# Maxima of the next head beside the scores of the running head: by key tiles in place of an even spread

## The chip, the cores and the metric

The kernel runs on one core of one Trainium2 chip. The metric is the device time of one execution in microseconds (us). The engines are TensorE (PE in the profile; PEld is its weight load), VectorE (DVE), ScalarE (ACT), GpSimd (POOL) and SyncE (SP), which issues DMAs.

## The reference, cut to what matters

The reference is one transformer block: a modulated layer norm, causal attention with 16 heads of 32 channels, a residual, and a mixture of experts. The part in question is the attention:

```python
B, T, C, H = (4, 2048, 512, 16)
qkv = x @ Wqkv.T + bqkv
q, k, v = (to_heads(z) for z in split(qkv, 3))
q, k = _rope(q), _rope(k)
att = jnp.einsum('bhqd,bhkd->bhqk', q, k) * scale
att = jnp.where(causal, att, -jnp.inf)
att = jax.nn.softmax(att, axis=-1)
y = jnp.einsum('bhqk,bhkd->bhqd', att, v)
```

The softmax needs the maximum of each query's row of scores before it can take exponentials.

## The kernel before, in words

**Batches and phases.** A loop runs over the 4 batches. In each, `front()` sets the order of the projections and `stream()` that of the attention; then comes the routing of tokens. The experts follow after all batches. `STEPS = front() + stream()` is one list of steps, and every engine walks the same list and does its own part of each step. So the list sets the order on each engine's in-order queue, and semaphores set the rest.

**Two passes over the scores of a head.** Scores are computed twice. In the first pass (`max` steps) the queries lie on the partitions: TensorE multiplies 128 queries by up to 512 keys into one of three PSUM banks `S1` (L1307), and VectorE reduces the bank to one maximum per query, with `reduce_max` (L1648) for whole tiles and with a masking operation (L1644) for the tiles on the diagonal, 128 to 512 wide. A head has 40 such tiles (`TILES`, `NTILE`), numbered by query block and then by chunk of 512 keys. After the 12th (`FIRST_HALF`) and the 40th, VectorE takes the maximum over chunks (`most`, L1654, it writes `mx`), TensorE transposes it (`row`, L1312, also into an `S1` bank), VectorE writes it negated to `mT` (`negated`, L1663), and SyncE copies it by a DMA (`max_row`, L736) into a row of `QK`. So the maximum is subtracted inside the second pass's matmul.

In the second pass (`score` steps) the keys lie on the partitions: TensorE multiplies 128 keys by 512 queries into one of three banks `S2` (L1330, with a masking matmul L1333 on the diagonal), and ScalarE takes the exponential into `Pt` (L1137). These 40 key tiles are taken in 15 rounds of two or three (`ROUNDS`, `NR`): rounds 0 and 1 (2 tiles each) belong to query chunk 0, rounds 2 to 4 (3, 2, 3) to chunk 1, rounds 5 to 8 (3 each) to chunk 2, rounds 9 to 14 (3, 3, 3, 3, 2, 2) to chunk 3. `ROUND_OF` gives the round of a tile. GpSimd adds the exponentials of a round (`plus`, L1002, into `Sm`), and TensorE multiplies them by the values (`value`, L1354, L1357, L1358), which also sums the denominators.

**The order.** `stream()` fills `beside`, a list of steps for each round of each head. Rounds are taken two at a time: one tile's score, then one step of `beside` of these two rounds, and so on until both are used up; then the two `plus`, then the two `value` steps of the two rounds before, then `closing` (copies of a finished chunk, and for every fourth head the joining of parts on GpSimd and the reciprocals of the denominators on VectorE, L1596). As 15 is odd, an even head's stretches begin at rounds 0, 2, 4 and so on, an odd head's at rounds 1, 3, 5, and the stretch "14, 0" holds the last round of an even head and the first of the odd one.

**Waits.** A `max` or `row` step on TensorE waits until the step three before it on the same bank has been read (L1261, L1263). A `row` waits for `most` (L1311). The scores of rounds 0 and 5 wait for the DMA of the row of their half (L1318). Q and K of head h+1 are brought by twelve DMAs (`stack`) that are issued once the scores of head h-1 are done, and the first `max` tiles of a chunk wait for theirs (L1306).

**Where the maxima stand before.** The maxima of head h are spread evenly over rounds of head h-1: for h = 1 over 12 steps from round 4, for later heads over 14 steps from round 2, three in most rounds and two in some. `most` comes one round after the last maximum of its half, `row` and `negated` two rounds after.

Of the kernel before, what the change touches and what calls it, by code (L numbers as in the profile page):

```python
# [89 lines left out]
NTILE = len(TILES)  # L90
SHAPES = ((2, 2), (3, 2, 3), (3, 3, 3, 3), (3, 3, 3, 3, 2, 2))
ROUNDS = [(j, tuple(range(sum(shape[:r]), sum(shape[:r + 1])))) for j, shape in enumerate(SHAPES) for r in range(len(shape))]
NR = len(ROUNDS)
# [13 lines left out]
def tile_at(j, k):  # L107

    return 2 * j * (j + 1) + k
# [7 lines left out]
ROUND_OF = {tile_at(j, k): r for r, (j, ks) in enumerate(ROUNDS) for k in ks}  # L117
# [34 lines left out]

FIRST_HALF = sum(qb < NT // 2 for qb, _, _ in TILES)
LAST_CHUNK = sum(qb < NT - TPC for qb, _, _ in TILES) + 8
TILES_FROM = 2
FIRST_TILES_FROM = 4
OUT_AT = (10, 10, 11, 12, 13, 14, 15, 16)


def stream():  # L160

    closing = [[] for _ in range(NR * H + 12)]
    beside = [[] for _ in range(NR * H)]
    negated = {}
    for i in range(LAST_CHUNK, NTILE):
        beside[(i - LAST_CHUNK) // 4].append(("max", 0, i))
    beside[2].append(("most", 0, 1))
    beside[3] += [("row", 0, 1), ("negated", 0, 1)]
    for hh in range(1, H):
        late = TILES_FROM if hh > 1 else FIRST_TILES_FROM  # L170
        at, span = NR * (hh - 1) + late, NR + 1 - late
        for i in range(NTILE):
            beside[at + i * span // NTILE].append(("max", hh, i))
            if i in (FIRST_HALF - 1, NTILE - 1):
                half, n = int(i >= FIRST_HALF), at + i * span // NTILE
                beside[n + 1].append(("most", hh, half))
                beside[n + 2].insert(0, ("row", hh, half))
                negated[n + 2] = ("negated", hh, half)
    for n, step in negated.items():
        beside[n].insert(2, step)  # L180
    for hh in range(H):
        for j in range(NCH):
            n = NR * hh + LAST_ROUND[j] + LAG
            closing[n].append(("copy", hh, j))
            if hh == H - 1 and j < NCH - 1:
                closing[n + 2] += [("join", NG - 1, j), *(("inverse", NG - 1, j, i) for i in range(TPC))]
                closing[n + 3].append(("scale", NG - 1, j))
            elif hh % GH == GH - 1 and hh < H - 1:
                closing[n + 3].append(("join", hh // GH, j))
                for i in range(TPC):  # L190
                    closing[n + 3 + i // 2].append(("inverse", hh // GH, j, i))
                closing[n + 5].append(("scale", hh // GH, j))
    last = NR * (H - 1)
    for i, t in enumerate(OUT_AT):
        closing[last + t].append(("out", *divmod(i, TPC)))
        if i == TPC - 1:
            closing[last + t].append(("moments",))
    closing[last + NR].append(("normed",))
    closing[NR * (H - 3)].append(("fold",))
    closing[last - 1].append(("widen", 0))  # L200
    closing[last + 5].append(("widen", 1))
    out = []
    for n in range(0, NR * H + 12, 2):
        if n < NR * H:
            here = [divmod(n, NR), divmod(n + 1, NR)]
            tiles = [("score", hh, r, k) for hh, r in here for k in ROUNDS[r][1]]
            aside = beside[n] + beside[n + 1]
            for i in range(max(len(tiles), len(aside))):
                out += tiles[i:i + 1] + aside[i:i + 1]
            out += [("plus", *of) for of in here]  # L210
        if 2 <= n < NR * H + 2:
            out += [("value", *divmod(n - 2, NR)), ("value", *divmod(n - 1, NR))]
        out += closing[n] + closing[n + 1]
    return out
# [8 lines left out]


STEPS = front() + stream()
USES = [step for step in STEPS if step[0] in ("max", "row")]
EMPTIED = {step: n + 1 for n, step in enumerate(step for step in STEPS if step[0] in ("max", "vproj"))}
# [1652 lines left out]
```

## Time and profile before

| | us |
|---|---|
| median of 3 runs | 4263.35 |
| lowest, highest | 4261.73, 4266.28 |
| the profiled execution | 4274.07 |
| its span, from first to last instruction | 4272.3 |

| engine | busy us | share of the span |
|---|---|---|
| TensorE matmuls | 3856.6 | 90% |
| VectorE | 2747.9 | 64% |
| ScalarE | 1806.0 | 42% |
| GpSimd | 2783.0 | 65% |

The mean granted clock of TensorE is 0.946 of 2.4 GHz. The profile is one execution. Matmuls are pipelined and their ends are modelled, so the start-to-start distance of two matmuls says more than their length: a matmul of 512 columns is 0.40 us long in the rows while the next starts 0.23 us later. A wait in a row stands in brackets with what ended it; on TensorE it is shorter than the distance between the two starts.

### The profile page before, as it was taken

The page shows a single profiled execution, that of the slowest core. Times are in us where ns is not written, and L with a number is a line of the kernel's source. Part 1 is how long each engine was busy: PE and PEld are TensorE (multiplying, and loading weights), DVE is VectorE, ACT ScalarE, POOL GpSimd, SP SyncE. Part 2 cuts the span into 40 slices and gives each one's busy share as a digit, 9 for nine tenths or more (in the row PEclk, how much of TensorE's full clock was granted, in tenths as well). Part 3 has the DMA queues.
Part 4 walks back from the last instruction along what each step waited for, and adds up shares of the span by engine and source line. Part 5 has one row for each costly group of instructions (what it writes and reads, how often), then busy time and mean ns, then how long its engine had stood idle before and what let it go on. Part 6 is the DMA issues. An engine that isn't in the chain of part 4 may idle for free. (4 is left out here: it accounts for less than half of the span.)

```text
span 4272.3 us, 80797 instructions
## 1 busy us (share of the span) xinstructions
PE 3856.6 (90%) x21344; PEld 2337.9 (55%) x21344; DVE 2747.9 (64%) x5841; ACT 1806.0 (42%) x3526; POOL 2783.0 (65%) x2251
## 2 busy tenths in 40 slices
PE   5989999987999999878899999879899999859998
PEld 2754544456744454457554454457545544547776
DVE  3767677466757767476667776467676774645655
ACT  1345555523355555332355555233455554311111
POOL 3768788824668879716678888427687888115554
PEclk8989999998999999989899999889999999979999
DMA  6533333243533333334433333425433332349997
GB/s 211 178 120 90 92 98 106 81 174 105 175 97 100 83 102 99 120 135 147 140 91 98 101 96 108 156 72 180 123 91 91 100 106 85 103 126 258 257 258 190
DMA packets 305439, 549.11 MB, mean 129 GB/s; under 512 B 59877, under 2 KB 99941, under 8 KB 301797
## 3 DMA queue, kind: packets, MB, share of 16 engines
q1 hardware_dynamic: 283496, 485.62, 37.8%
q0 software_dynamic: 21504, 58.40, 5.9%
q8 instruction: 183, 3.00, 0.3%
q14 instruction: 256, 2.09, 0.2%
HBM read 311.86 MB, written 174.85 MB: 114 GB/s over the span
## 5 line engine op out<-in xcount | busy, mean ns | idle before, releaser
L1137 ACT ACTIVATE Pt<-PS 128x512 f32<-128x512 f32 (+3 forms) x2560 | 1205.2, 542 | 1003.0 <-PE PS L1330 557.5
L1002 POOL TENSOR_TENSOR Sm<-Pt 128x512 f32<-128x512 f32 (+3 forms) x960 | 1028.4, 1077 | 389.2 <-ACT Pt L1137 383.2
L1648 DVE TENSOR_REDUCE part<-PS 128x1 f32<-128x512 f32 x1536 | 1004.2, 685 | 335.6 <-PE PS L1307 330.5
L1307 PE MATMUL PS<-QK 96*128 96x512 f32 (+3 forms) x2560 | 1026.6, 419 | 84.1 <-DVE mT L1663 24.8
L1330 PE MATMUL PS<-QK 97*128 97x512 f32 (+3 forms) x2560 | 994.2, 410 | 40.8 <-DMA QK<-mT 20.9
L1354 PE MATMUL PS<-Pt,V 128*32 128x512 f32 (+3 forms) x5120 | 874.4, 556 | 37.1 <-POOL Sm L1002 36.9
L1358 PE MATMUL PS<-Sm,onesv 128*32 128x512 f32 (+3 forms) x1920 | 823.2, 537 | 0.0
L1644 DVE CUSTOM_DVE_ANT_0 PS<-PS,consts 128x128 f32<-128x128 f32 (+3 forms) x1024 | 504.0, 495 | 411.1 <-PE PS L1307 403.8
L1330 PEld LDWEIGHTS PS<-QK 97*128 97x128 f32 x2560 | 489.6, 194 | 478.3 <-issue 349.6
L1002 POOL TENSOR_TENSOR Sm<-Sm,Pt 128x512 f32<-128x512 f32 (+1 forms) x640 | 712.4, 1113 | 50.2
L1307 PEld LDWEIGHTS PS<-QK 96*128 96x128 f32 x2560 | 496.0, 195 | 292.3 <-DVE part L1648 107.6
L1354 PEld LDWEIGHTS PS<-Pt,V 128*32 128x32 f32 x5120 | 218.5, 111 | 364.5 <-issue 243.3
L1291 PE MATMUL PS<-hTu,W 128*128 128x512 f32 x1024 | 327.9, 402 | 25.2 <-DVEq L644 13.4
L976 POOL TENSOR_TENSOR t<-qraw,cs 128x1024 f32<-128x1024 f32 x64 | 183.7, 2870 | 171.3 <-ACT qraw L1102 162.1
L1038 POOL DMA_INDIRECT out<-z,it x96 | 138.9, 1447 | 214.9 <-issue 111.8
L1596 DVE RECIPROCAL den<-den 128x128 f32<-128x128 f32 x256 | 221.2, 914 | 73.6 <-DMA den<-od 72.1
L1456 PEld LDWEIGHTS PS<-XT,Wg 128*96 128x96 f32 x1536 | 251.6, 164 | 27.0 <-issue 25.4
L1456 PE MATMUL PS<-XT,Wg 128*96 128x192 f32 x1536 | 260.5, 328 | 1.3 <-ACT XT L1188 1.3
L1333 PE MATMUL PS<-mtbf,idbf 128*128 128x128 bf16 (+1 forms) x1024 | 238.7, 236 | 0.0
L1291 PEld LDWEIGHTS PS<-hTu,W 128*128 128x128 f32 x1024 | 194.4, 193 | 72.4 <-issue 17.1
L1124 ACT ACTIVATE od<-PS 128x512 f32<-128x512 f32 x256 | 155.8, 609 | 138.5 <-PE PS L1358 138.5
L1102 ACT ACTIVATE qraw<-PS,bqg 128x512 f32<-128x512 f32 x128 | 87.0, 680 | 284.3 <-PE PS L1291 248.5
(169 smaller groups left out, 4945.7 us busy)
## 6 DMA issues: line engine op xcount, KB each, us to landing
QK<-qkd SPq DMA_DIRECT2D x720, 128.0 KB, 3.1
qkd<-st SPq DMA_DIRECT2D x64, 1024.0 KB, 4.5
Wg<-wgu SPq DMA_DIRECT2D x48, 768.0 KB, 5.0
o<-od SPq DMA_DIRECT2D x448, 64.0 KB, 2.0
W<-wd SPq DMA_DIRECT2D x3, 6144.0 KB, 21.5
Wd<-wdn SPq DMA_DIRECT2D x48, 384.0 KB, 6.0
xin<-x SPq DMA_DIRECT2D x16, 1024.0 KB, 7.8
vd<-vst SPq DMA_DIRECT2D x16, 1024.0 KB, 6.2
```

Source lines behind the costliest of these rows:

```text
L1002: nc.gpsimd.tensor_tensor(total, of[0][:, first:CH] if i == 1 else total, of[i][:, first:CH], ALU.add).then_inc(sum_done, 1)
L1137: nc.scalar.activation(Pt[:, t % NPT, first:CH], S2[t % NS2][:, first:CH], ACT.Exp, scale=SCALE).then_inc(exp_done, 1)
L1291: last = mm(bank, W[:, w, k, i, g * P:(g + 1) * P], (hTu, hTl)[h][:, j % 2, k], start=(k, w, h) == (0, *TERMS[0]), stop=(k, w, h) == (KT - ...
L1307: mm(s1[:, 0:w], QK[0:3 * HD, hh % 2, 0, qb * P:(qb + 1) * P], QK[0:3 * HD, hh % 2, 1, c * CH:c * CH + w], start=True, stop=True).then_inc ...
L1330: last = mm(S2[t % NS2][:, first:CH], QK[0:3 * HD + 1, hh % 2, 1, k * P:(k + 1) * P], QK[0:3 * HD + 1, hh % 2, 0, j * CH + first:(j + 1) * ...
L1333: last = mm(S2[t % NS2][:, first:first + masked], idbf[:, :], mtbf[:, 2 * P - masked:2 * P], start=False, stop=True)
L1354: mm(O[j % 2][i * HD:(i + 1) * HD, firsts[i]:CH], V[:, g % 2, k, h * HD:(h + 1) * HD], of[i][:, firsts[i]:CH], start=begins, stop=r == LAS ...
L1358: mm(O[j % 2][3 * HD:P, firsts[1]:CH], onesv[:, :], Sm[:, at % NSM, firsts[1]:CH], start=begins, stop=r == LAST_ROUND[j]).then_inc(pv_done, 1)
L1456: last = mm(banks[i][:, q, :], Wg[:, u % HELD, k, o:o + HALF], XT[:, u % 2, k // 2, k % 2, :], start=k == 0, stop=k == KT - 1)
L1596: v.reciprocal(den[:, cols], den[:, cols]).then_inc(den_inv, 1)
L1644: v.tensor_tensor_reduce(out=s1[:, 0:w], in0=s1[:, 0:w], in1=K[:, K_NEG + CH - w:K_NEG + CH], scale=1.0, scalar=-3e38, op0=ALU.add, op1=AL ...
L1648: v.reduce_max(part[:, qb, cc:cc + 1], s1[:, 0:w], AX.X).then_inc(s1_dve, 1)
```

## The change

For heads from 2 on, maximum i of head h goes to the round that holds tile i + 4 of head h-1 (`AHEAD`), so that there is one maximum for each score; the last four fall into rounds 0 and 1 of head h itself. For head 1 the maxima keep their even spread. For all heads from 1 on `most` stands in the round of the last maximum of its half and no longer in the next, and `row` and `negated` one round after it and no longer two. The rows are put in after all maxima are placed, at the head of their round. For heads from 2 on this gives, for the first half, the last maximum in round 6 in place of 5, for the second half in round 1 of the next head in place of round 0; the rows stay in the rounds 7 and 2. For head 1 `most` and the rows stand a round earlier.

```diff
-TILES_FROM = 2
-FIRST_TILES_FROM = 4
+AHEAD, FIRST_TILES_FROM = 4, 4
...
-    negated = {}
+    negated, rows_at = {}, []
...
     for hh in range(1, H):
-        late = TILES_FROM if hh > 1 else FIRST_TILES_FROM
-        at, span = NR * (hh - 1) + late, NR + 1 - late
         for i in range(NTILE):
-            beside[at + i * span // NTILE].append(("max", hh, i))
+            if hh == 1:
+                n = FIRST_TILES_FROM + i * (NR + 1 - FIRST_TILES_FROM) // NTILE
+            else:
+                past, tile = divmod(i + AHEAD, NTILE)
+                n = NR * (hh - 1 + past) + ROUND_OF[tile]
+            beside[n].append(("max", hh, i))
             if i in (FIRST_HALF - 1, NTILE - 1):
-                half, n = int(i >= FIRST_HALF), at + i * span // NTILE
-                beside[n + 1].append(("most", hh, half))
-                beside[n + 2].insert(0, ("row", hh, half))
-                negated[n + 2] = ("negated", hh, half)
+                half = int(i >= FIRST_HALF)
+                beside[n].append(("most", hh, half))
+                rows_at.append((n + 1, hh, half))
+    for n, hh, half in rows_at:
+        beside[n].insert(0, ("row", hh, half))
+        negated[n] = ("negated", hh, half)
     for n, step in negated.items():
         beside[n].insert(2, step)
```

As the code then emits them, the stretch of rounds 1, 2 of an odd head reads before and after (S score, M maximum of the head running ahead, tile numbers behind):

```
before  S.2 most S.3 row  S.0 M0  S.1 negated S.2 M1 M2
after   S.2 M38 S.3 M39  S.0 most  S.1 row  S.2 M0 negated M1 M2
```

## Rows read from the trace of the kernel before

**Rows 1.** The page, part 1: busy us (share) of each engine, xinstructions

```profile
PE 3856.6 (90%) x21344; PEld 2337.9 (55%) x21344; DVE 2747.9 (64%) x5841; ACT 1806.0 (42%) x3526; POOL 2783.0 (65%) x2251
```

**Rows 2.** TensorE's waits: who <- for whom: us in total, times, longest

```profile
PE PS L1354 <- POOL Sm L1002: 36.9, 25, 4.5
...
PE PS L1307 <- DVE mT L1663: 24.8, 33, 0.9
PE PS L1307 <- DVE part L1644: 24.4, 45, 1.3
PE PS L1330 <- DMA QK<-mT: 20.9, 4, 5.5
```

**Rows 3.** Windows: us, busy by engine, PEclk, DMA, GB/s; three of heads 4, 5

```profile
1329.95:1333.15 3.20, 3.20 (x30) 2.23 (x26) 2.16 (x5) 1.66 (x4) 3.12 (x5) 1.00 0.80 203
...
1368.35:1373.53 5.18, 3.76 (x28) 2.02 (x26) 1.60 (x7) 2.73 (x6) 1.35 (x2) 1.00 0.67 189
...
1397.26:1402.50 5.24, 5.03 (x34) 2.14 (x30) 3.56 (x7) 1.60 (x4) 4.58 (x5) 1.00 0.43 102
```

**Rows 4.** Groups by line, weight loads: xcount, busy us, mean ns, idle before

```profile
L1307 PEld LDWEIGHTS PS<-QK 96*128 96x128 f32 x2560 | 496.0, 195 | 292.3 <-DVE part L1648 107.6 <-DVE part L1644 66.8 <-DVE mT L1663 46.7
```

**Rows 5.** Timeline, TensorE, rounds 12, 13: start, us, operation, xcount [wait]

```profile
1359.39 0.40 PE L1307 MATMUL PS<-QK 96*128 96x512 f32 x1
1359.62 0.40 PE L1330 MATMUL PS<-QK 97*128 97x512 f32 x1
```

**Rows 6.** Timeline, VectorE, to the end of rounds 14, 0 (head 6)

```profile
511.52 1.88 DVE L1648 TENSOR_REDUCE part<-PS 128x1 f32<-128x512 f32 x3
513.32 0.69 DVE L1644 CUSTOM_DVE_ANT_0 PS<-PS,consts 128x512 f32<-128x512 f32 x1
...
514.11 0.19 DVE L1654 TENSOR_REDUCE mx<-part 128x8 f32<-128x32 f32 x1
```

**Rows 7.** Timeline, TensorE, rounds 13, 14 (head 5), the last maxima

```profile
1399.08 1.63 PE L1307 MATMUL PS<-QK 96*128 96x384 f32 x3
1400.65 0.63 PE L1354 MATMUL PS<-Pt,V 128*32 128x512 f32 x3
```

**Rows 8.** Timeline, TensorE, rounds 2, 3 (head 4), the last maxima

```profile
1335.22 0.98 PE L1307 MATMUL PS<-QK 96*128 96x384 f32 x3
1336.51 0.33 PE L1307 MATMUL PS<-QK 96*128 96x128 f32 x1 [0.30 <-DVE part L1644]
1336.87 0.62 PE L1354 MATMUL PS<-Pt,V 128*32 128x512 f32 x2
```

**Rows 9.** Timeline, TensorE, rounds 6, 7 (head 4), the last maximum

```profile
1347.32 0.39 PE L1307 MATMUL PS<-QK 96*128 96x256 f32 x1 [0.85 <-DVE mT L1663]
```

**Rows 10.** Timeline, TensorE, rounds 13, 14 (head 3), a value

```profile
1328.96 0.63 PE L1354 MATMUL PS<-Pt,V 128*32 128x512 f32 x3 [1.25 <-POOL Sm L1002]
```

**Rows 11.** Windows, rounds 1, 2, heads 3 to 13: one, the 24's sum

```profile
514.55:518.18 3.63, 3.63 (x27) 2.13 (x25) 1.61 (x7) 2.73 (x6) 1.22 (x2) 1.00 0.76 216
...
sum 102.54, PE 91.97 PEld 48.74 DVE 38.46 ACT 65.72 POOL 46.81; mean PE 3.83 PEld 2.03 DVE 1.60 ACT 2.74 POOL 1.95
```

**Rows 12.** Timeline, all engines, the first head's rounds 2, 3

```profile
1175.31 0.19 DVE L1654 TENSOR_REDUCE mx<-part 128x8 f32<-128x32 f32 x1
...
1175.55 0.38 PE L1312 MATMUL PS<-consts,mx 128*8 128x128 f32 x1 [0.43 <-DVE mx L1654]
```

**Rows 13.** Timeline, TensorE, rounds 1, 2 (head 5), the third maximum

```profile
1371.73 0.44 PE L1307 MATMUL PS<-QK 96*128 96x384 f32 x1
```

**Rows 14.** Timeline, TensorE, rounds 3, 4 (head 13), a value

```profile
746.32 0.63 PE L1354 MATMUL PS<-Pt,V 128*32 128x512 f32 x3 [1.37 <-POOL Sm L1002]
```

**Rows 15.** Windows, rounds 3, 4 of head 5, first batch

```profile
446.39:451.70 5.31, 5.31 (x33) 3.10 (x31) 3.28 (x9) 2.83 (x6) 3.55 (x4) 0.80 0.31 82
```

**Rows 16.** Windows, rounds 9, 10 of head 3 in two batches

```profile
383.66:391.33 7.67, 6.42 (x34) 3.15 (x30) 7.57 (x14) 3.26 (x6) 7.11 (x8) 0.78 0.12 27
...
1311.90:1318.21 6.31, 5.07 (x34) 2.66 (x31) 6.31 (x13) 3.20 (x6) 6.15 (x7) 1.00 0.16 36
```

## The prediction

> **What bounds the kernel now.** I began with the page. TensorE is busy 90% of the span, the next engines 65% and 64% [rows 1], and most of its work is the stream of attention. So the place to look is what TensorE waits for there. The list of waits gives little: 24.8 us for `negated` (L1663), 24.4 us for the diagonal maxima (L1644), 36.9 us for GpSimd's sums, and 20.9 us for a row's DMA, in four waits [rows 2]. Better placed maxima can't take away much more than the first two.
>
> Next I cut the stream into stretches of two rounds, as the code emits them (scores and maxima mixed, then two values): fifteen for two heads. In heads 4 and 5 of the second batch all run at full clock, and the reader is to see that lengths follow counts: 4 scores with 2 maxima take 3.20 us, 4 with 6 take 5.24 [rows 3]. So I price each stretch by itself. One maximum more or less on an unstalled TensorE I take as 0.235 us: its weight load is 0.195 us whatever the width [rows 4], the bound from below, and the wait-free steps from maximum to score in a run of full ones are 0.23 (1359.39 to 1359.62 [rows 5]). On VectorE a full maximum costs 0.60 us, for three follow each other in 1.88 and a fourth begins 1.80 behind the first, though one is 0.69 long [rows 6]. So on a run of maxima VectorE is the slower, with three PSUM banks between the two.
>
> The Trainium skill, "TensorE: Matmul & The Clock Gate", section "Wait — 56ns, not 53.3ns?", gives a matmul's spacing as columns over 2.4 GHz plus 2.5 ns, 56 ns for a 128-wide one. By it, dropping a 128-wide maximum would return 0.06 us and not 0.235; the trace has no such spacing between two maxima of the stream. No other sentence uses it.
>
> **The change part by part.** The maxima of a pair of heads' stretches become 4 5 6 6 6 6 5 4 (first, even head) and 5 5 6 6 6 6 4, in place of 2 6 6 6 5 6 6 5 and 3 6 6 5 6 6 6. From head 2 on the last maximum of a half falls one round later, its row in the round it had. No operation is added or removed. Per batch seven even heads (2 to 14) and seven odd ones (1 to 13) change, and head 15 at its start.
>
> *Stretches that shorten.* (a) Rounds 13, 14: the last three maxima take 1.57 us up to the value, because two wait for banks; without two of them the value stands some 0.6 behind: 0.97 less [rows 7]. (b) Rounds 2, 3: the sixth maximum waits until 1336.51 and the value begins at 1336.87; the fifth is the last of three that begin at 1335.22 and take 0.98, so it starts at about 1335.7, and without the sixth the value stands 0.43 behind it: 0.7 less [rows 8]. (c) Rounds 6, 7: `negated` lies behind a full maximum and holds a bank, 0.85 us of idle time [rows 9]; a 128-wide one takes that place, but a full one more stands ahead of `most`: 0.34 less. (d) One maximum less in rounds 12, 13, in 14, 0 and in 3, 4: 0.25 each. *That lengthen.* (e) Rounds 0, 1: two more, 0.46. (f) Rounds 8, 9: one more, 0.28. (g) Rounds 7, 8: one more, and the last now waits for the bank of a full one: 0.55. Rounds 4, 5, 5, 6, 9 to 12 keep their count: nothing.
>
> *Where the cover is gone.* In heads 3, 7, 11 GpSimd also joins the group's parts, and a value in rounds 13, 14 waits 1.25 us for its sum [rows 10]: there (a) and (g) come to nothing, the wait for GpSimd takes their place. In heads 4, 8, 12 reciprocals stand ahead of `negated`: (b) is half.
>
> Per batch: even heads -7 x 0.34 (c) - 7 x 0.5 (d) + 7 x 0.46 (e) + 7 x 0.28 (f) - 4 x 0.7 - 3 x 0.35 (b) = -4.6; odd heads -7 x 0.25 (d) - 4 x (0.97 - 0.55) = -3.4. Together -8.0 us.
>
> *The added wait.* Rounds 1, 2 of odd heads. Before, `most` begins at 514.11 [rows 6], ahead of the stretch (514.55 to 518.18, 3.63 us [rows 11]), and the row goes out at 515.04 unhindered. After, both last maxima lie in this stretch. The first is made 0.27 in, VectorE takes it at 0.89 (0.6 behind, as ever), the second at 1.49; `most` begins 0.79 later (514.11 against 513.32 [rows 6]) and ends at 2.47; the row, behind three scores in TensorE's queue, goes at 2.52, though TensorE is free at 1.45. That a row starts 0.05 behind the end of `most` is seen in the first head [rows 12]. Behind it wait a score and three maxima; `negated` comes behind the first of these and frees the third's bank at 3.87. From that third maximum to the end it is 1.80 us, as in head 5 (1371.73 to 1373.53 [rows 13]): 5.67. Before, these 24 stretches (heads 3 to 13) took 102.54 us, 4.27 each [rows 11]: in some the next head's first maximum waits for its DMA, and that wait is now hidden. So +1.40 x 6, and +1.2 in head 15: +9.6 per batch. Bounds for one: 5.3 (if VectorE is quicker to the last maxima) and 6.0.
>
> *What takes it up.* In head 13 a value of rounds 3, 4 waits 1.37 us for GpSimd, which folds the output weights [rows 14]; in head 15 it waits likewise. A later TensorE finds these done: -1.3 and -1.2. Head 5's falls of the clock behind its DMA wait go too: two of four stretches of rounds 3, 4 took 5.3 us at a lower clock [rows 15] and not 4.4, so -0.5. Sum per batch: -8.0 + 9.6 - 3.0 = -1.4, in four -6 us.
>
> *The clock.* In rounds 9, 10 of heads 3, 7, 11 TensorE idles for a maximum, 1.3 us at the longest [rows 2]. Nine of these twelve stretches show a lower granted clock (0.78: part of the stretch at 1.2 GHz) and take some 7.67 us, three stay at 2.4 GHz and take 6.31: 1.37 dearer [rows 16]. The new idle time is 1.07 us at the row and 0.5 at the bank, among narrow matmuls. I take a fall in two of three: 16 x 1.37 = 22, less 2 for falls that go. Bounds: 0 and 24 x 1.37 = 33.
>
> *Queues.* SyncE issues a row's DMA behind twelve for Q and K, and behind it the copies of the head before; it waited for `negated` before and still does. TensorE waits for a row's DMA four times, once in each batch, in the first head [rows 2], whose rows don't move. In even heads the way from the last score of the head before to the score that needs the row shrinks by 1.2 us (the terms a, b, e), in odd heads it grows. I put nothing; if the even ones had no slack it would be 7 x 4 x 1.2 = 34 us, but then some of today's heads would wait too.
>
> Total: -6 + 20 = +14 us. The profiled execution took 4274.07 us (span 4272.3), 10.7 above the median of the runs; the sum is a difference, and on the median it gives 4263 + 14, some 4276.
>
> **Rivals.** (1) *The clock holds.* If the idle time in rounds 1, 2 doesn't lower it, -6 us stays: 4257. For it: rounds 1, 2 of head 5 took 5.18 us with a long DMA wait, at full clock [rows 3]. Against it: [rows 16]. The Trainium skill, same page, "HAM oscillation — how this bites in real kernels", asks for longer idle gaps than these before the clock falls; by it this rival would be the forecast. (2) *The row hardly waits.* If rounds 1, 2 take 5.3 and (b) and (c) return the whole of their waits (0.5 more in 28 stretches), 24 x 0.37 + 28 x 0.5 = 23 us go: 4253 from the forecast, 4234 from rival 1. It decides where VectorE reaches a maximum clearly less than 0.6 us behind TensorE; no row shows that. (3) *GpSimd takes the gain in all heads.* In rounds 13, 14 it is busy 4.58 of 5.24 us without holding TensorE [rows 3]; at 4.27 it would, and 0.31 of 0.97 is lost, 16 x 0.31 = 5 us; with a fall of the clock in all 24 (11 more) this gives 4292, and if the whole 0.97 is lost 4302. (4) *Nothing to be told*: a maximum moved is one placed elsewhere, and the waits only change place: 4263.
>
> **How the numbers follow.** Forecast 0.5, rival 1 0.2, rival 2 0.1, rival 3 0.15, rival 4 0.05. The range, 4252 to 4294, leaves out the far parts of 2 and 3. Less than 0.2% (8.5 us) can't be told from no change. Faster (under 4254.8): rival 2 and part of 1, 0.18. Within: the rest of 1, rival 4 and the low side of the forecast, 0.27. Slower (over 4271.9): 0.55.
>
> **What would show it.** Right: a wait of the row's transpose for `mx`, about 1.0 us, in odd heads 3 to 15 and hardly elsewhere in the stream; rounds 1, 2 at 5.4 to 6.0 us at full clock; a lower granted clock behind about two thirds of them; rounds 13, 14 at 4.3 in heads 1, 5, 9, 13; rounds 0, 1 at 3.65; the wait for `negated` in rounds 6, 7 under 0.6; the DMA wait for Q and K gone. Wrong: if the clock stays up the sum is 20 us too high, and if rounds 1, 2 stay near 4 us another 35.

## The result, and the profile after

The changed kernel takes 4313 us in the median (4296 to 4317 in four runs, 4314 in four further ones), the kernel before 4264 to 4268: slower by a ratio of 1.0095 (95% interval 1.008 to 1.011), in the later comparison 1.0112 (1.0086 to 1.0139). The direction was forecast, the size was not: +47 to +49 us where I had +14, and outside the range, whose end was 4294.

The first profiled run of the changed kernel, 4295.94 us (span 4294.1), is the quickest of the eight, with a mean granted clock of 0.945. Most of its runs have 0.940 to 0.942. So I took a second trace, of a run of 4315.98 us at 0.940 (E5), and one of the kernel before at 4270.86 us and 0.948 (E6, its first had 0.946 and 4274.07). "First" and "second trace" below mean these. A "fall" is a stretch of two rounds whose granted clock (the PEclk column) is below 1.00; a "place" is one such stretch in one head and batch.

TensorE's waits after the change, first trace, columns as in [rows 2]; lines from L1307 on stand four further down than before:

```profile
PE PS L1358 <- POOL Sm L1006: 55.4, 47, 4.5
...
PE PS L1316 <- DVE mx L1658: 27.6, 32, 1.2
...
PE PS L1311 <- DVE part L1648: 15.3, 17, 1.2
...
PE PS L1311 <- DVE mT L1667: 13.5, 24, 0.9
...
PE PS L1311 <- DVE part L1652: 11.8, 39, 0.8
...
PE PS L1311 <- DMA QK<-qkd: 2.8, 5, 0.8
```

The reader is to see two things. The waits that the change aimed at shrank ([rows 2]: `negated` 24.8 to 13.5, the diagonal maxima 24.4 to 15.3), though the wait for whole tiles grew from 4.4 to 11.8, and a new one stands there, the row's transpose for `mx`, 27.6 us. The wait for a head's DMA went from 10.5 us to 2.8. And GpSimd's sums went from 36.9 us in 25 waits to 55.4 in 47.

The stretches of two rounds in heads 4 and 5 of the second batch, to be laid beside [rows 3]; in order rounds 0, 1, then 8, 9 of head 4, and 1, 2, then 3, 4, then 7, 8, then 13, 14 of head 5:

```profile
1336.10:1339.82 3.72, 3.72 (x33) 2.47 (x29) 2.69 (x7) 1.73 (x4) 3.64 (x5) 1.00 0.79 212
...
1354.87:1359.82 4.95, 4.95 (x34) 2.42 (x32) 4.28 (x10) 2.62 (x6) 4.87 (x5) 1.00 0.24 57
...
1373.98:1379.68 5.70, 4.25 (x29) 2.37 (x27) 3.09 (x11) 2.90 (x6) 2.25 (x4) 1.00 0.69 182
1379.68:1383.71 4.03, 4.03 (x33) 2.33 (x31) 2.55 (x8) 2.72 (x6) 2.86 (x4) 1.00 0.46 120
...
1388.49:1394.26 5.77, 5.56 (x35) 2.78 (x34) 3.43 (x10) 2.90 (x7) 5.61 (x6) 1.00 0.13 33
...
1403.77:1408.11 4.34, 4.24 (x33) 1.67 (x29) 2.42 (x5) 1.60 (x4) 4.26 (x5) 1.00 0.39 88
```

Rounds 1, 2 take 5.70 us (5.67 forecast) and rounds 13, 14 take 4.34 (4.27). TensorE's timeline in rounds 1, 2 of head 5 has both new waits in it, at the row and at a bank:

```profile
1374.99 0.63 PE L1334 MATMUL PS<-QK 97*128 97x512 f32 x2
1376.51 0.27 PE L1316 MATMUL PS<-consts,mx 128*8 128x128 f32 x1 [0.89 <-DVE mx L1658]
...
1377.88 0.44 PE L1311 MATMUL PS<-QK 96*128 96x384 f32 x1 [0.57 <-DVE mT L1667]
```

and VectorE's has the chain that makes the row late, two maxima of 0.6 us and then `most`:

```profile
1374.87 0.69 DVE L1652 TENSOR_REDUCE part<-PS 128x1 f32<-128x512 f32 x1 [1.72 <-PE PS L1311]
1375.48 0.69 DVE L1648 CUSTOM_DVE_ANT_0 PS<-PS,consts 128x512 f32<-128x512 f32 x1
...
1376.27 0.19 DVE L1658 TENSOR_REDUCE mx<-part 128x8 f32<-128x32 f32 x1
```

Two of the 24 stretches of rounds 1, 2, heads 3 to 13, first trace, and their sum:

```profile
1521.36:1528.13 6.77, 5.31 (x30) 2.57 (x28) 3.09 (x11) 2.90 (x6) 3.06 (x4) 0.84 0.77 206
...
3300.79:3308.42 7.63, 5.71 (x30) 2.77 (x28) 3.05 (x11) 2.94 (x6) 2.99 (x3) 0.73 0.63 171
...
sum 152.08, PE 116.42 PEld 59.69 DVE 74.02 ACT 69.83 POOL 78.97; mean PE 4.85 PEld 2.49 DVE 3.08 ACT 2.91 POOL 3.29
```

[rows 11] had 102.54 for these. With the wait, 11 stay at 1.00 and near 5.7 us, and 13 show a lower granted clock.

### The profile page after: what moved, and what is told of

Read it like the earlier page. It is cut to its first block and busy times, and to the rows that moved or that the text cites. A ratio compares the mean times of both kernels' runs of the same rounds, so it can differ in the third digit from the quotient of the medians.

```text
span 4294.1 us, 80797 instructions
## 1 busy us (share of the span) xinstructions
PE 3856.5 (90%) x21344; PEld 2340.2 (54%) x21344; DVE 2755.2 (64%) x5841; ACT 1807.1 (42%) x3526; POOL 2784.6 (65%) x2251
## 5 line engine op out<-in xcount | busy, mean ns | idle before, releaser
L1311 PE MATMUL PS<-QK 96*128 96x512 f32 (+3 forms) x2560 | 1036.8, 419 | 62.0 <-DVE part L1648 15.3
L1358 PE MATMUL PS<-Pt,V 128*32 128x512 f32 (+3 forms) x5120 | 879.8, 556 | 56.4 <-POOL Sm L1006 55.4
L1600 DVE RECIPROCAL den<-den 128x128 f32<-128x128 f32 x256 | 221.2, 914 | 57.0 <-DMA den<-od 55.4
```

The lines of the kernel that those rows point to most:

```text
L1311: mm(s1[:, 0:w], QK[0:3 * HD, hh % 2, 0, qb * P:(qb + 1) * P], QK[0:3 * HD, hh % 2, 1, c * CH:c * CH + w], start=True, stop=True).then_inc ...
L1358: mm(O[j % 2][i * HD:(i + 1) * HD, firsts[i]:CH], V[:, g % 2, k, h * HD:(h + 1) * HD], of[i][:, firsts[i]:CH], start=begins, stop=r == LAS ...
L1600: v.reciprocal(den[:, cols], den[:, cols]).then_inc(den_inv, 1)
```

## Experiments

The theory I took to the chip: the late row is the whole loss, with its wait and the falls of the clock behind it. Rival A: the loss beyond the first trace's +22 us comes from some other place, heads 3, 7, 11 for one. Times are medians; before in the same runs was 4267 to 4268.

**E1, no late row.** The last two maxima and `most` of odd heads back in round 0, the row out a round sooner:

```diff
                 n = NR * (hh - 1 + past) + ROUND_OF[tile]
+                if hh % 2:
+                    n = min(n, NR * hh)
```

> The changed kernel, but the last two maxima and `most` of odd heads stay in round 0, and their second row goes out in round 1 (as many steps as before, only placed otherwise). Theory (the late row in rounds 1, 2 of the odd heads, its wait and the falls of the clock behind it, is the whole loss): no wait of the row's transpose for `mx` in heads 3 to 15, rounds 1, 2 back at 3.6 to 4.3 us, their granted clock at 1.00, rounds 14, 0 longer by 0.7 to 1.2 us. In the trace after stands 22 us over before; without the 54 of rounds 1, 2 and with 24 x 0.9 in rounds 14, 0 this is -11: some 4253 us, with the timed runs as near to it as those of before are. Rival A (the loss beyond the trace's 22 us comes from elsewhere: heads 3, 7, 11 with GpSimd in rounds 13, 14, or other places): the runs keep 25 us more, some 4280. Rival B (only the wait costs, the clock falls anyhow): 4268.

Measured 4249.3 us, ratio 0.9964 (0.9951 to 0.9976): below before, as the theory had it. Windows of rounds 14, 0 of head 4 and, in another row, 1, 2 of head 11 (second batch), with the 24 stretches' sum:

```profile
1352.50:1357.50 5.00, 4.95 (x34) 2.36 (x31) 3.81 (x9) 1.85 (x4) 4.08 (x5) 1.00 1.02 273
...
1573.26:1576.65 3.39, 3.39 (x27) 1.94 (x25) 1.67 (x7) 2.73 (x6) 0.97 (x2) 1.00 0.61 168
...
sum 81.38, PE 81.17 PEld 46.83 DVE 40.23 ACT 65.34 POOL 33.72; mean PE 3.38 PEld 1.95 DVE 1.68 ACT 2.72 POOL 1.40
```

No fall is left there, and rounds 14, 0 take 5.00 us where the changed kernel takes 4.08: 0.92 more, 0.9 expected. The falls in heads 3, 7, 11, which the second trace will show (E5), are nearly gone too, although this edit leaves those places alone. Twelve windows there, rounds 9 to 1 around the maxima of heads 4, 8, 12:

```profile
sum 261.64, PE 230.74 PEld 116.58 DVE 230.46 ACT 121.58 POOL 247.82; mean PE 19.23 PEld 9.71 DVE 19.20 ACT 10.13 POOL 20.65
```

In the second trace of the changed kernel they take 283.38.

**E2, the row one round later.** Maxima as in the change, `row` and `negated` of the second half in round 3:

```diff
-                rows_at.append((n + 1, hh, half))
+                rows_at.append((n + 1 + (hh > 1 and hh % 2 and half), hh, half))
```

> The changed kernel, but `row` and `negated` of the second half of odd heads from 3 on stand one round later, in round 3. All maxima stay where the change put them. Theory: TensorE finds `mx` ready, rounds 1, 2 of odd heads take 4.3 to 4.5 us instead of 5.7 to 7.6 (-51 us over 24), rounds 3, 4 get the row (0.2 each, +5) and some of the waits that the late TensorE no longer covers (+12): -16 against before, some 4248 us. Rival A (loss from elsewhere): some 4275. Rival C (the row, one round later, comes too late for the score that reads it): a wait of a score for its DMA in round 5 of odd heads, up to 1 us each, +24: 4272, and a fall of the clock behind it makes it more.

Measured 4260.3 us, ratio 0.9984 (0.9975 to 0.9994), 12 us above the theory. Rounds 1, 2 did what it said:

```profile
sum 103.92, PE 95.96 PEld 53.62 DVE 68.48 ACT 67.95 POOL 46.10; mean PE 4.00 PEld 2.23 DVE 2.85 ACT 2.83 POOL 1.92
```

and no score waits in round 5, so rival C is out. The 12 us are elsewhere. One of three such stretches of rounds 0, 1 in heads 4, 8 and 12:

```profile
400.14:407.00 6.86, 6.86 (x33) 4.18 (x29) 4.50 (x8) 1.86 (x4) 4.83 (x6) 0.50 0.56 157
```

At full clock it takes 3.72, so the three make up 9 us of the trace. They come behind rounds 13, 14 of heads 3, 7, 11, a place for which I had put no cost at all.

**E3, the wait filled with work.** Four matmuls into the row's own bank, overwritten by the transpose, ahead of its wait:

```diff
                         _, hh, half = step
+                        if hh > 1 and hh % 2 and half:
+                            for _ in range(4):
+                                mm(s1, QK[0:3 * HD, hh % 2, 0, 0:P], QK[0:3 * HD, hh % 2, 1, 0:CH], start=True, stop=True)
                         pe.wait_ge(max_all, ONE + 2 * (H * b + hh) + half + 1)
```

> The changed kernel with four more matmuls (97 rows, 512 columns, into the row's own bank, overwritten after) ahead of the row's transpose in odd heads from 3 on: TensorE works through most of the 1.07 us in which it otherwise waits for `mx`. They add no time of their own where the wait is. Theory (falls of the clock behind this wait are the larger part of the loss): no lower granted clock in rounds 1, 2, these stay at 5.6 to 5.9 us; the 13 falls there (1.4 us each) go from the trace, 18 us, and some 24 x 1.4 = 33 from the timed runs: 4280. Rival B (the wait alone costs): 4313, as the changed kernel. Rival D (the matmuls come behind the wait or make VectorE's maxima later): over 4313.

Measured 4267.9 us, ratio 1.0001 (0.9992 to 1.0009): 46 us are gone although TensorE has work added, 12 more than the 33 or so that I expected. One of the 24 stretches (head 9) and their sum:

```profile
1509.83:1515.54 5.71, 5.14 (x34) 3.13 (x32) 3.09 (x11) 2.90 (x6) 2.27 (x4) 1.00 0.71 202
...
sum 136.94, PE 122.85 PEld 74.46 DVE 74.02 ACT 69.82 POOL 68.33; mean PE 5.12 PEld 3.10 DVE 3.08 ACT 2.91 POOL 2.85
```

The stretch is as long as before at full clock (5.70), but no one of 24 shows a lower clock. So the idle time brought these falls on, not the row or its place. Rival B is out. The sum also gives the wait without the clock: 136.94 less 102.54 [rows 11] is 34.4 us, 33.6 forecast.

**E4, the late maxima alone.** The kernel before, with the last two maxima of odd heads in round 1:

```diff
-            beside[at + i * span // NTILE].append(("max", hh, i))
+            n = at + i * span // NTILE
+            after = hh > 1 and hh % 2 and i >= NTILE - 2
+            beside[n + after].append(("max", hh, i))
```

> The kernel before, with one thing of the change alone: the last two maxima of odd heads from 3 on stand in round 1, not 0 (`most`, `row`, `negated` in the rounds they had). Theory: rounds 1, 2 grow by 1.4 us for the wait and in half of them or more by another 1.4 for the clock; round 0 loses 2 x 0.235. 24 x (1.4 - 0.47) = 22, + 13 to 24 x 1.4 = 18 to 33, less some 12 that rounds 3, 4 take up: +28 to +43, some 4300 us. Rival A (this step costs only what is in the trace of after, the rest of the loss is elsewhere): 4275. Rival B (no clock falls): 4274.

Measured 4301.8 us, ratio 1.0082 (1.0069 to 1.0095), as expected. Its wait for the row and its 24 stretches, 13 of them with a fall:

```profile
PE PS L1314 <- DVE mx L1656: 27.7, 32, 1.2
```

```profile
sum 148.83, PE 112.66 PEld 57.72 DVE 74.00 ACT 69.83 POOL 81.49; mean PE 4.69 PEld 2.40 DVE 3.08 ACT 2.91 POOL 3.40
```

**E5 and E6, second traces of the two kernels**, unchanged.

> The changed kernel itself, once more, for a second trace and for its times beside those of the other runs. In its first trace (4296 us, mean granted clock 0.945) 13 of the 24 stretches of rounds 1, 2 in odd heads have a fall of the clock; its other three runs took 4312 to 4317 at 0.940 and 0.941. Theory: the time follows the number of falls behind the row's wait, all 24 stretches have the same wait of 0.9 us, and at 0.941 the trace shows some 24 more low pieces of 3.4 us than before (it was 4 more at 0.945), most in rounds 1, 2, and stretches without a fall are as long as in the first trace (5.70, 4.03, 3.73). Rival A: at 4313 us the falls in rounds 1, 2 are again some 13 and full-clock stretches are longer somewhere.

> The kernel before, once more, for a second trace. Its first one stood at a mean clock of 0.946 and 4274 us, while most of its runs have 0.950 and 4267. Theory: at 0.950 the trace has about 10 low pieces fewer than the 136 of the first, and each stretch without a fall has the length that it has in the first trace (3.20, 5.24, 4.40, 3.63 to 4.10). Rival: the same number of falls, other lengths.

E5: 4313.9 us in the median, 4299.3 to 4328.9, and the time goes with the mean clock (0.945, 0.942, 0.940, 0.936 from the quickest to the slowest). Half of the theory held. Behind the row's wait 16 of 24 stretches fell, not all. These 24 and the rounds 3, 4 behind them are 28.5 us longer than E3's, in which none fell (155.79 against 136.94, and 108.72 against 99.11). The rest of the difference to the first trace is in heads 3, 7 and 11. Windows of rounds 13, 14 and, behind each, 0, 1; head 7 of the second batch, then head 3 of the third:

```profile
1480.01:1486.51 6.50, 4.31 (x33) 1.67 (x29) 4.89 (x9) 1.60 (x4) 6.34 (x6) 1.00 0.53 128
1486.51:1490.23 3.72, 3.72 (x32) 2.47 (x29) 2.68 (x7) 1.73 (x4) 3.64 (x5) 1.00 0.95 245
2261.46:2268.80 7.34, 5.16 (x33) 1.71 (x29) 5.03 (x9) 1.59 (x4) 7.18 (x7) 0.84 0.53 143
2268.80:2275.65 6.85, 6.85 (x32) 4.17 (x28) 4.49 (x8) 1.86 (x4) 4.82 (x6) 0.50 0.53 157
```

The same work takes 10.22 us or 14.19. In the second pair the granted clock falls behind the values' wait, and stays down to the end of rounds 0, 1. TensorE's timeline there, and GpSimd's:

```profile
2264.36 0.63 PE L1358 MATMUL PS<-Pt,V 128*32 128x512 f32 x3 [0.67 <-POOL Sm L1006]
...
2266.93 1.07 PE L1358 MATMUL PS<-Pt,V 128*32 128x512 f32 x3 [1.51 <-POOL Sm L1006]
```

```profile
2261.66 1.29 POOL L1006 TENSOR_TENSOR Sm<-Pt 128x512 f32<-128x512 f32 x1
2263.03 1.27 POOL L1006 TENSOR_TENSOR Sm<-Sm,Pt 128x512 f32<-128x512 f32 x1
2264.27 1.27 POOL L1006 TENSOR_TENSOR Sm<-Pt 128x512 f32<-128x512 f32 x1
2265.62 1.26 POOL L1006 TENSOR_TENSOR Sm<-Sm,Pt 128x512 f32<-128x512 f32 x1
2266.84 1.27 POOL L946 TENSOR_TENSOR ot<-ot,den 128x512 f32<-128x512 f32 x1
```

GpSimd adds without a pause, some 1.3 us each, and each value starts just behind the second sum that it needs. It is the bound here. TensorE with two maxima less only idles more: 2.18 us in two waits, where before it was 1.25 at most [rows 10]. In the second trace 7 of the 12 places fall (5 of them through all of rounds 0, 1), in the first 3 (one of them so), in the two traces of before none of 24. The rounds 9 to 1 about these places, twelve windows together, before (first trace) and in the second trace of after:

```profile
sum 256.99, PE 232.10 PEld 117.45 DVE 237.53 ACT 120.80 POOL 248.06; mean PE 19.34 PEld 9.79 DVE 19.79 ACT 10.07 POOL 20.67
```

```profile
sum 283.38, PE 242.57 PEld 122.80 DVE 237.72 ACT 123.03 POOL 259.70; mean PE 20.21 PEld 10.23 DVE 19.81 ACT 10.25 POOL 21.64
```

So +26 us, and +11 in the first trace (267.68); 6.4 of each are the two maxima more in rounds 0, 1 (e). E6, a single run of 4270.9 us, has the lengths of the first trace of before in stretches that don't fall, and three falls fewer in rounds 1, 2 (the 24: 99.82 against 102.54). In low pieces as the expectations count them, E5 has 18 more than the first trace of before (24 expected), E6 6 fewer (10 expected).

**E7, half the filling.** As E3 with two matmuls in place of four:

```diff
-                            for _ in range(4):
+                            for _ in range(2):
```

> As the filled kernel (changed kernel, matmuls ahead of the row's transpose), with two matmuls in place of four: some 0.45 us of idle time is left of 0.9. If the fall of the clock answers to the length of the idle time, few falls or none come in rounds 1, 2 and the time is that of the filled kernel, 4268 us; if any wait there brings them on, 13 or more remain and it takes 4290 to 4313. I expect the first, with up to 8 falls, 4268 to 4280. If the matmuls themselves made the filled kernel quicker in some other way than by the clock, half of them give half of it: 4290.

Measured 4292.3 us, ratio 1.005 (1.003 to 1.0069), 4275 to 4298, and not the 4268 to 4280 that I expected. By the number alone that is the rival's "half of it". The trace, of the slowest run, says otherwise. The wait is 0.42 us now, and stretches without a fall are as long as in E3 (5.70):

```profile
1372.24 0.63 PE L1317 MATMUL PS<-QK 96*128 96x512 f32 x2
1373.30 0.27 PE L1319 MATMUL PS<-consts,mx 128*8 128x128 f32 x1 [0.42 <-DVE mx L1661]
```

6 of 24 stretches still fall (sum 144.69, in E3 136.94), and 7 of the 12 places in heads 3, 7, 11 do, which the matmuls don't touch, against 2 in E3's trace. So falls at the row answer to the length of the idle time, none of 24 at 0, 6 at 0.4 and 11 to 16 at 0.9 (four traces, E9 with them). Of E3's 46 us 28.5 are the row's. The rest is no luck of one trace, for E3's eleven runs all lie between 4262.6 and 4272.1. It is in heads 3, 7, 11, and comes with the filled wait though the matmuls stand elsewhere; the twelve windows in E3's trace, against 283.38 in the second:

```profile
sum 262.35, PE 228.32 PEld 115.53 DVE 229.55 ACT 121.86 POOL 249.42; mean PE 19.03 PEld 9.63 DVE 19.13 ACT 10.15 POOL 20.79
```

**E9, only heads 3, 7, 11 repaired.** The changed kernel, row still late, with two of the last four maxima of heads 4, 8, 12 back in round 14:

```diff
                 n = NR * (hh - 1 + past) + ROUND_OF[tile]
+                if hh % GH == 0 and i < NTILE - 2:
+                    n = min(n, NR * hh - 1)
```

> The changed kernel (with its late row and its wait), in which only heads 4, 8, 12 have two of their last maxima back in round 14 of heads 3, 7, 11, beside GpSimd's joining. In the two traces of the changed kernel rounds 9 to 1 around these twelve places take 267.7 and 283.4 us together, in those of before 257.0 and 256.1, in the early kernel with this repair 255.1: TensorE reaches the values of rounds 13, 14 sooner, waits for GpSimd twice (0.67 and 1.51 us) and in up to five of twelve the clock falls for 10.2 us, which costs 4 us each. Theory (this is the second cause of the loss, beside the row's wait): the twelve come back to some 256, no long fall is left there, and the time drops by 11 to 27 us from 4313: some 4294, the rest of the loss staying in rounds 1, 2. Rival (the row's wait alone is the loss, the other only moves with it): only the 6.4 us of rounds 0, 1 go, 4307.

Measured 4286.5 us, ratio 1.0056 (1.0042 to 1.0069), 27 us below the changed kernel; the rival's 4307 is out. The twelve windows of rounds 9 to 1 in its trace:

```profile
3162.78:3183.73 20.95, 18.42 (x119) 9.38 (x115) 19.57 (x38) 10.16 (x21) 19.93 (x19) 1.00 0.33 92
...
sum 254.83, PE 224.69 PEld 114.07 DVE 235.47 ACT 121.31 POOL 241.79; mean PE 18.72 PEld 9.51 DVE 19.62 ACT 10.11 POOL 20.15
```

GpSimd is busy 19.93 of 20.95 us, and two more maxima on TensorE cost nothing. No long fall came behind rounds 13, 14, one short one did. Of the 27 us 6.4 are the two maxima that no longer stand in rounds 0, 1; some 20 are the falls.

**E8, both repairs**, E1's and E9's.

> The early kernel (4249 us), with two of the four maxima of heads 4, 8, 12 that it has in round 0 put back into round 14 of heads 3, 7, 11, where GpSimd joins the group. If GpSimd sets the end of those rounds whatever TensorE has to do (prediction: the gain there is nil), the two cost nothing there (12 stretches of rounds 13, 14 stay at the 5.64 us of the early kernel on average) and rounds 0, 1 give back 12 x 0.53 = 6.4 us: 4243. Rival: TensorE's own work sets it, the 12 stretches go back to the 6.00 of before (+4.3) or longer, and the sum is -2 to +3: 4247 to 4252. The waits for GpSimd's sums there, 0.9 or 0.67 and 1.51 in the early kernel, should fall below 0.7 in both.

Measured 4241.8 us, ratio 0.9948 (0.9935 to 0.9962): the quickest of all, 25 us under the kernel before and 7.5 under E1. The twelve windows sum to 255.12, 6.5 less than in E1. I was wrong in two things. Where the clock holds in rounds 9, 10, the wait for GpSimd in 13, 14 is still 0.98 to 1.07 us and not below 0.7. And rounds 13, 14 of these heads take 5.95 us on average, near the rival's 6.00 and not E1's 5.64; 7 places fell in rounds 9, 10 and not 10 as in E1, which gives the time back. So the same repair is worth 27 us with the late row (the changed kernel to E9) and 7.5 without it (E1 to E8): most of the falls in heads 3, 7, 11 come together with the row's wait. Not all do, for E2 has three of them without it.

**E10, one maximum more in rounds 12, 13.** E8, with one maximum of odd heads moved out of round 14:

```diff
+                if hh > 1 and hh % 2 and i == NTILE - 6:
+                    n = NR * hh - 2
```

> The early kernel with the repair in heads 4, 8, 12 (4242 us), in which odd heads from 3 on have one maximum (512 wide) in round 13 and not in round 14: rounds 12, 13 get six instead of five, rounds 14, 0 five instead of six. From the traces: rounds 14, 0 go from 5.00 us to 4.4 (28 stretches, less 0.6), rounds 12, 13 from 4.02 to 4.4 (16 stretches, 0.4 more) and stay as they are in heads 4, 8, 12, where the value waits 0.4 us for GpSimd anyway. 24 x 0.6 - 12 x 0.4 = 9 us less: 4233. Rival: the last maximum and `most` come no sooner, the row's place in round 1 is early enough in both, and the sixth maximum in rounds 12, 13 makes the value wait as it did before the change; then 4240 to 4245.

Measured 4243.4 us, ratio 0.9952 (0.9939 to 0.9966): no gain over E8, the rival's time. Rounds 14, 0 gave 17 us and rounds 12, 13 took 7, as expected. But its waits for a head's DMA, 2.9 us in E8's trace, are

```profile
PE PS L1317 <- DMA QK<-qkd: 6.2, 13, 0.7
```

the 24 stretches of rounds 1, 2 grew from 81.81 to 86.83 us, and TensorE waits 1.6 us for GpSimd in head 15 where it waited 1.0: a TensorE that comes sooner finds the next thing late.

## Why the prediction was half right

The prediction's terms against the second traces (four batches, us; each is the difference between the two traces' windows of one kind over the heads that the term names; where a stretch has a fall, its length without one is taken from another trace of like kind, and the rest counts in the rows on the clock and on rounds 9 to 1):

| term | forecast | measured |
|---|---|---|
| (a) rounds 13, 14, other heads | -15.5 | -16 |
| (b) rounds 2, 3 | -15.4 | -18 |
| (c) rounds 6, 7 | -9.5 | -7 |
| (d) rounds 12, 13; 14, 0; 3, 4 | -21 | -25 |
| (e) rounds 0, 1 | +12.9 | +15 |
| (f) rounds 8, 9 | +7.8 | +5 |
| (g) rounds 7, 8 | +8.8 | +17 |
| row's wait, heads 3 to 15 | +38.4 | +43 |
| taken up in rounds 3, 4 | -12 | -8 |
| clock behind the row's wait, less falls that go | +20 | +21 |
| rounds 9 to 1 of heads 3, 7, 11, beyond (e) | 0 | +21 |
| stretches put at nothing: 4, 5 (-4.7), 5, 6 (+3.5), heads 0 and 1 | 0 | -3 |

The right column sums to +45, as the second traces differ (4315.98 less 4270.86). The first traces differ by 22: three falls fewer behind the row's wait, more falls in the trace of before, and +4 for rounds 9 to 1 of heads 3, 7, 11.

*Right.* The row's wait: 0.89 us where I had 1.07, the bank 0.57 where I had 0.5, the stretch 5.70 against 5.67. Of 24 stretches 13 and 16 fall behind it, where I had 16. But a fall costs 1.8 us with its part in rounds 3, 4 (28.5 over 16), and not 1.37. In return some 15 us of falls go and not 2, half of them in head 15, where rounds 9, 10 then grow by 7.3, so that 8 are left. The term is met by two errors that cancel, which is luck. The placement prices (a) to (f) are each within 4 us; their sum was forecast at -41 and is -46. E4 shows the row's part by itself, E1 and E3 take it out, and most of the falls in heads 3, 7, 11 go with it. Rival 1 falls with the PEclk column, rival 2 with the 5.70 us. The Trainium skill, "TensorE: Matmul & The Clock Gate", section "HAM oscillation — how this bites in real kernels", which asks for longer idle gaps, would have had the clock hold; the traces differ from it (falls behind waits of 0.89 and 0.57 us), and the measurement decides.

*A reading that was wrong, at little cost.* I took a maximum as 0.235 us whatever its width. Rounds 11, 12 of head 1 before the change have a narrow one between two scores:

```profile
317.89 0.40 PE L1330 MATMUL PS<-QK 97*128 97x512 f32 x1
318.12 0.23 PE L1307 MATMUL PS<-QK 96*128 96x128 f32 x1
318.19 0.45 PE L1330 MATMUL PS<-QK 97*128 97x512 f32 x1
```

The score starts 0.06 us behind it (0.07 by the rounded times), as in 60 places of that trace. So a 128-wide maximum without a wait costs less than a full one.

*Where the sum failed.* It is the sentence "there (a) and (g) come to nothing, the wait for GpSimd takes their place". For (a) it was true of the time at full clock, and I stopped there: 0.97 us of work that turns into idle time is not a zero, if that idle time stands among the few matmuls that are left. [rows 10] showed a wait of 1.25 us there, which had brought no fall; without the two maxima it becomes 2.18 in two waits. I had just priced falls behind 1.07 at the row, and I didn't lay one beside the other. What the runs showed in its place is +21 us in rounds 9 to 1 of these heads beyond (e). E9 shows it: the same row wait, two maxima back as cover, and 27 us go, 6.4 of them (e). But the cost isn't independent of the row's wait: without that wait the same two maxima bring 7.5 (E1 to E8). Rival 3 was the nearest to it in words and named the other heads, not these. For (g) it was false: rounds 7, 8 grow by 0.6 us in these heads too, which GpSimd doesn't absorb (+7).

*Why it came out at +47 and not at the +22 of the first traces.* The first trace of each kernel was an unusual run: of after one with few falls, of before one with more than most. One trace settles the length of a stretch at full clock to a few hundredths, and the count of falls hardly at all.

What stays open: why some of these places fall and others don't, and how the row's wait bears on them. Six traces have the maxima of heads 4, 8, 12 as the change put them (first, second, E1, E2, E3, E7). Of their 72 places in heads 3, 7, 11, 33 fell in rounds 9, 10, and none of these in 13, 14; of the 39 that kept their clock in 9, 10, 23 fell in 13, 14. A fall in 9, 10 makes TensorE later and shortens the idle time that follows (to some 0.3 and 1.5 us, or to one wait of 0.8 to 1.5, from 0.67 and 1.51). And falls in 9, 10 are rarer where rounds 1, 2 have a wait for the row: 2 to 4 of 12 in the first, the second, E4, E7 and E9, against 7 to 10 in all other traces, those of before included. That ties the two costs together; why a wait some 20 us earlier should do this no run shows, and it is no strict rule: in E2, without that wait, 3 of the 5 places that kept their clock in 9, 10 fell.

## What to carry to other kernels

Work taken off TensorE where it waits for another engine turns into idle time, and that can cost more than the work did (some 20 us of falls here, with the late row): price each moved step twice, at full clock and by the idle time that it leaves. Leave a reduction a round's lead over the matmul that reads its result; here that was worth 45 us (E9 to E8). Count falls of the clock in more than one trace before a difference is put down to anything else.

## What the runs showed of the hardware

Idle times of 0.89 (0.98 in the fourth batch) and 0.57 us in a stretch of 5.70 us lowered the granted clock in 11 to 16 of 24 places in each of four traces (first, second, E4, E9); 0.42 and 0.57 in 6 of 24, 0.57 alone in none. Idle times of 0.67 and 1.51 us ahead of two values lowered it in up to 7 of 12, five times through all of the next stretch, at 1.2 GHz, where 3.72 us became 6.85. One piece of 0.97 to 1.25 us in the same place (before, E4, E8, E9, E10) lowered it in 3 of 33. And a fall can cost next to nothing: in rounds 9, 10 of heads 3, 7, 11 it adds 1.37 us there [rows 16], but in the two traces of before rounds 9 to 1 together take 21.1 to 21.8 us with it (21.5 on average) and 21.1 to 21.3 (21.2) without, since GpSimd, busy 20.5 to 20.8 us of them, sets their end.
